# Setup work moved behind the first norm, value rows of the first image ahead of its depthwise product, and six of its first 16 stack transfers issued by GpSimd

## The reference

```python
# x = x + _L0_conv_ref(_ln_c(x), ...)
y = jnp.einsum('nchw,oc->nohw', x, cv1_w) + cv1_b[None, :, None, None]
t = y.transpose(0, 2, 3, 1)
v = (t @ vp_w.T + vp_b).reshape(B, H, W, G, GC)                 # values
dw = jax.lax.conv_general_dilated(y, dw_w, (1, 1), 'SAME', feature_group_count=C, ...)
dw = dw + dw_b[None, :, None, None]                             # depthwise 3x3
om = dw.transpose(0, 2, 3, 1) @ om_w.T + om_b                   # offsets and masks
...                                                             # split off, mask
d = _dcn_core(v, off, mask) @ op_w.T                            # bilinear samples of v at 9 taps
z = d @ cv2_w.T
z = (z - bn_m) * (bn_g / jnp.sqrt(bn_v + EPS)) + bn_b
z = z * jax.nn.sigmoid(z)
```

## Time and profile before

| What | Value |
|---|---|
| Median of 3 runs | 918.97 us (918.94 to 920.76) |
| The profiled execution, its own time | 918.25 us |
| Its span | 916.4 us |
| PE busy | 599.2 us (65%) |
| DVE busy | 538.9 us (59%) |
| ACT busy | 322.0 us (35%) |
| POOL busy | 465.7 us (51%) |
| First tap product on PE starts | 51.88 us |
| First add on POOL starts | 57.86 us |
| Mean granted clock of TensorE | 0.743 |

### The profile page before, as it was taken

The page is one execution under the profiler, slowest core; times in us unless marked ns, Lnnn a source line. Parts: engine busy times, 40 slices in busy tenths (PEclk is TensorE's granted clock), DMA queues, the critical chain, the costliest instruction groups (busy, mean ns, idle before and its releaser), DMA issues.

```text
span 916.4 us, 10354 instructions
## 1 busy us (share of the span) xinstructions
PE 599.2 (65%) x3032; PEld 446.3 (49%) x3032; DVE 538.9 (59%) x1018; ACT 322.0 (35%) x536; POOL 465.7 (51%) x364
## 2 busy tenths in 40 slices
PE   1566878787878787761288888873867771656511
PEld 0445556565656565640265665652656661445300
DVE  3257878797969796962366566552564654444411
ACT  2435352525252525100154554551232320433400
POOL 0058988899989998996100000004575733000075
PEclk9967575758585858555599999986686875677755
DMA  9463526565556562600445455410010101445311
GB/s 359 145 151 80 144 58 150 167 146 171 142 163 151 168 145 68 151 0 23 153 129 160 151 159 171 147 45 15 12 30 23 30 15 33 128 129 138 100 33 37
DMA packets 67013, 101.22 MB, mean 110 GB/s; under 512 B 25742, under 2 KB 45198, under 8 KB 66958
## 3 DMA queue, kind: packets, MB, share of 16 engines
q1 hardware_dynamic: 62416, 93.07, 35.7%
q0 software_dynamic: 4096, 6.30, 2.6%
q10 hardware_dynamic: 446, 1.20, 0.4%
HBM read 37.67 MB, written 25.10 MB: 68 GB/s over the span
## 4 chain that ended last, share of the span: by engine, by line
PE 32%; DVE 19%; issue 18%; POOL 13%; ACT 9%; SPq 5%; DMA 4%; POOLq 0%; DVEq 0%; ACTq 0%
DVE sb_prod L1085 6%; POOL sb_yg L1382 5%; POOL xs L1363 5%; PE ps_pa L479 4%; PE ps_t L514 4%; PE ps_c L472 3%; PE ps_t L581 2%; PE ps_pb L599 2%; DVE sb_hats L1160 2%; DVE sb_hats L1071 2%; ACT sb_hats L859 2%; PE ps_t L582 1%; PE ps_t L590 1%; PE ps_t L589 1%; PE ps_c L499 1%
## 5 line engine op out<-in xcount | busy, mean ns | idle before, releaser
L1351 POOL TENSOR_TENSOR sb_acc<-sb_acc,sb_prod 128x1024 f32<-128x1024 f32 x128 | 300.2, 2376 | 12.0 <-DVE sb_prod L1085 11.7
L1382 POOL DMA_INDIRECT sb_yg<-ys,sb_jdx x64 | 61.4, 959 | 295.3 <-DMA ys<-sb_yt 277.3
L514 PE MATMUL ps_t<-sb_vbd,sb_hx 128*128 128x256 f32 x576 | 139.9, 391 | 69.9 <-DVE sb_prod L1085 57.8
L1085 DVE TENSOR_TENSOR sb_prod<-ps_t,sb_hy 128x1024 f32<-128x1024 f32 x128 | 153.6, 1216 | 41.7 <-PE ps_t L514 31.9
L514 PEld LDWEIGHTS ps_t<-sb_vbd,sb_hx 128*128 128x128 f32 x576 | 110.1, 267 | 100.2 <-DVE sb_prod L1085 70.1
L1363 POOL DMA_INDIRECT xs<-sb_xr,sb_idx x64 | 64.4, 1007 | 25.4 <-issue 15.8
L1213 DVE TENSOR_TENSOR sb_hid<-ps_t,sb_hid 114x512 f32<-114x512 f32 x69 | 46.4, 686 | 46.3 <-ACT sb_hid L880 41.0
L499 PE MATMUL ps_c<-sb_dwT,sb_omx 128*128 128x256 f32 x144 | 53.5, 527 | 14.8 <-DVE sb_hats L1071 10.2
L880 ACT ACTIVATE sb_hid<-ps_t 114x512 f32<-114x512 f32 x69 | 41.2, 599 | 48.0 <-PE ps_t L582 47.9
L499 PEld LDWEIGHTS ps_c<-sb_dwT,sb_omx 128*128 128x128 f32 x144 | 34.9, 259 | 23.3 <-issue 17.4
L479 PE MATMUL ps_pa<-sb_ypad,sb_diag 128*64 128x256 f32 x96 | 40.8, 599 | 8.2 <-ACT sb_yrep L781 8.2
(11 more groups left out here) (253 smaller groups left out, 1294.2 us busy)
## 6 DMA issues: line engine op xcount, KB each, us to landing
sb_hx<-sb_hats SPq DMA_DIRECT2D x384, 96.0 KB, 2.2
xs<-sb_x3t SPq DMA_DIRECT2D x32, 512.0 KB, 6.1
sb_acc<-in_wcat SPq DMA_DIRECT2D x16, 876.0 KB, 4.5
sb_yrep<-in_wcat SPq DMA_DIRECT2D x7, 876.0 KB, 4.5
sb_nt<-xs SPq DMA_DIRECT2D x32, 128.0 KB, 2.1
sb_acc<-in_ucat SPq DMA_DIRECT2D x22, 160.0 KB, 2.4
sb_xt<-xs SPq DMA_DIRECT2D x23, 128.0 KB, 2.2
ys<-sb_yt SPq DMA_DIRECT2D x16, 128.0 KB, 2.4
```

The costliest lines, as they stand in the source:

```text
L514: last = mm(tb[u % 2][:, j * 256:(j + 1) * 256], hx[q % 3][:, j, o:o + P], vbd[n % 2][:, j * 256:(j + 1) * 256], start=True, stop=True)
L1085: v.tensor_tensor(o.rearrange("p (g c q) -> p g c q", g=G, q=H), tb[u % 2][:, :].rearrange("p (g c q) -> p g c q", g=G, q=H), w, ALU.mult) ...
L1351: g.tensor_tensor(acc[n % 2][:, t, :], acc[n % 2][:, t, :], prod[a % 3][:, :], ALU.add).then_inc(s_pool_acc, 1)
L1382: g.indirect_dma_start(out=yg[b][:, t, z, :], out_offset=None, in_=ys[0:NJT[m] * TILE, :], in_offset=bass.IndirectOffsetOnAxis(ap=jdx[m][: ...
```

## The change

Four things are changed.

1. **Setup behind the norm.** The making of `diag`, of `bns`, and the copies to `run` move into two steps, `fold` and `folded`, that stand behind `cv1` of image 0 in the list; ACT's square root is in `fold`. The fills that need no constant move ahead of DVE's wait for the constants. PE no longer waits for `s_set` at the start but at the first depthwise row; ACT and POOL wait for 4 in place of 5; DVE waits for 5 inside `fold`, and for the constants there too.
2. **Values first.** For image 0 alone, `value_rows` and `values` stand ahead of the three `depthwise_row`, `depthwise` and `offsets`.
3. **GpSimd issues.** Of the 16 stack transfers of image 0's first group, POOL issues part 2 (4 transfers, after `hath`) and half of part 3 (2 transfers, after `hatl`), on a semaphore of their own, `s_hp`. SP issues the other 10. PE waits for both before the first tap; ACT waits for both before it writes `hath[0]` again (group 2).
4. **Order strings.** ACT's string has one letter more, DVE's two, POOL's 24 (its new step `columns` returns at once for all groups but the first). Otherwise every engine's steps stand in the same order as before.

The strings are shown by their first lines; the rest of each is the same order moved along by the added letters.

```diff
     "act": """
-        aaaaaaaaaa aaaaaaaapa papaaappaa aaaappappa appaaaaaap pappaappaa aaaappappa appaaaaaap pappaappaa aaaappappa appaaaappp
+        aaaaaaaaaa aaaaaaaaap apapaaappa aaaaappapp aappaaaaaa ppappaappa aaaaappapp aappaaaaaa ppappaappa aaaaappapp aappaaaapp
...
     "dve": """
-        aaaaaaaaat taatattttt tttataaata tatattttaa ttpattpttp ttptttataa atatatattp aattatpttt ppttppptat taaatatata ttpttaattt
+        aaaaaaaaaa attaatattt tttttataaa tatatatttt aattpattpt tpttptttat aaatatatat tpaattatpt ttppttpppt attaaatata tattpttaat
...
     "pool": """
-        ttaatttttt tttttttttt attttptttt tttttttttt aptttptttt tpsttttttt pttattttpt ttttpstttt tttpttattt tptttttpst ttttttptta
+        ttaaaaaaaa tttttttttt ttttttaaaa ttttttpttt ttttttttta aaaptttptt tttpsttttt ttpttaaaat tttptttttp stttttttpt taaaattttp
...
@@ -75,8 +75,10 @@
 
     conv, taps, post = [], [], []
     for n in range(B):
-        conv += [("x_tokens", n), ("stats", n, 0), ("norm", n, 0), ("xn_channels", n), ("cv1", n), *(("depthwise_row", n, i) for i in range(3)),
-                 ("depthwise", n), ("offsets", n), *(("value_rows", n, i) for i in range(4)), ("values", n), *column_group(n, 0), ("row_distances", n, 0), ("row_distances", n, 1), ("row_weights", n, 0),
+        depthwise = [*(("depthwise_row", n, i) for i in range(3)), ("depthwise", n), ("offsets", n)]
+        value = [*(("value_rows", n, i) for i in range(4)), ("values", n)]
+        conv += [("x_tokens", n), ("stats", n, 0), ("norm", n, 0), ("xn_channels", n), ("cv1", n)] + [("fold",), ("folded",)] * (n == 0)
+        conv += (value + depthwise if n == 0 else depthwise + value) + [*column_group(n, 0), ("row_distances", n, 0), ("row_distances", n, 1), ("row_weights", n, 0),
                  ("row_weights", n, 1), *column_group(n, 1), *column_group(n, 2)]
         taps += [("tap", n, k, t) for k in range(K) for t in range(TT)]
         post += [("sampled", n), ("z", n), ("x1", n), ("stats", n, 1), ("norm", n, 1)] + routing(n, 0)[:-1]
@@ -288,6 +290,11 @@
         h3 = [tb[b][:, 512:1024] for b in range(2)]
         ca, cc = cb[:, 0:512], cb[:, 512:1024]
 
+
+        s_hp = sem("s_hp")
+
+        def landed(q):
+            return 256 * (q // 3 + 1) - 96 * (q % 3 == 0)
 
         s_const, s_zero, s_set = map(sem, ("s_const", "s_zero", "s_set"))
         s_bn, s_act_bn, s_pe_comb, s_act_comb = map(sem, ("s_bn", "s_act_bn", "s_pe_comb", "s_act_comb"))
@@ -364,9 +371,11 @@
                     sp.wait_ge(s_pe_t, TRI * TT * (q - 2))
                 sp.wait_ge(s_act_hh, 3 * q + 3)
                 for part, src in ((0, hath[b]), (2, hath[b]), (1, hatl[b]), (3, hatl[b])):
+                    if q == 0 and part == 2:
+                        continue
                     if part == 1:
                         sp.wait_ge(s_dve_hl, q + 1)
-                    for j in range(NJ):
+                    for j in range(NJ // 2 if q == 0 and part == 3 else NJ):
                         sp.dma_start(hx[s][32 * part:32 * part + 32, j, :].bitcast(f32),
                                      src[32 * j:32 * j + 32, :].bitcast(f32)).then_inc(s_hx[s], 16)
 
@@ -475,6 +484,8 @@
             def depthwise_row(n, i):
                 if i == 0:
                     pe.wait_ge(s_act_yr, n + 1)
+                    if n == 0:
+                        pe.wait_ge(s_set, 5)
                 for a in range(2):
                     last = mm(pa[0:C, 0:PIX], diag[:, 2 * i + a, :], ypad[:, i:i + H, 2 * a:2 * a + W], start=(i == 0 and a == 0),
                               stop=(i == 2 and a == 1))
@@ -504,9 +515,11 @@
                 u = UNITS * n + k * TT + t
                 q = NTRI * n + k // TRI
                 if t == 0 and k % TRI == 0:
-                    pe.wait_ge(s_hx[q % 3], 256 * (q // 3 + 1))
+                    pe.wait_ge(s_hx[q % 3], landed(q))
                 if k == 0 and t == 0:
                     pe.wait_ge(s_dve_v, n + 1)
+                    if n == 0:
+                        pe.wait_ge(s_hp, 96)
                 if u >= 2:
                     pe.wait_ge(s_dve_p, u - 1)
                 for j in range(NJ):
@@ -752,7 +765,6 @@
                      "xn2_channels": xn2_channels, "queries": queries, "keys": keys, "attn_values": attn_values, "k_tokens": k_tokens, "context": context, "q_channels": q_channels,
                      "mix": mix, "attend": attend, "nx": nx_channels, "nup": nup, "ndown": ndown, "nout": nout, "x4": x4}
             pe.wait_ge(s_const, n_const)
-            pe.wait_ge(s_set, 5)
             mm(pb[0:C, 0:C], op_[:, :], cv2[:, :], start=True, stop=True).then_inc(s_pe_comb, 1)
             walk("pe", steps)
 
@@ -763,11 +775,13 @@
             for dst, name in consts[1::2]:
                 act.dma_start(dst, A[name]).then_inc(s_const, 16)
             act.wait_ge(s_const, n_const)
-            act.wait_ge(s_bn, 1)
-            af(bns[:, 1:2], bns[:, 0:1], ACT.Sqrt).then_inc(s_act_bn, 1)
             act.wait_ge(s_pe_comb, 1)
             af(opcv[:, :], pb[0:C, 0:C], ACT.Copy).then_inc(s_act_comb, 1)
-            act.wait_ge(s_set, 5)
+            act.wait_ge(s_set, 4)
+
+            def fold():
+                act.wait_ge(s_bn, 1)
+                af(bns[:, 1:2], bns[:, 0:1], ACT.Sqrt).then_inc(s_act_bn, 1)
 
             def xn_channels(n):
                 act.wait_ge(s_pe_xnt, n + 1)
@@ -812,7 +826,9 @@
                 af(cb[:, 0:TRI * PIX], cb[:, 0:TRI * PIX], ACT.Relu, scale=-1.0, bias=1.0).then_inc(s_act_hh, 1)
                 act.wait_ge(s_act_hh, 3 * q + 2)
                 if q >= 2:
-                    act.wait_ge(s_hx[(q - 2) % 3], 256 * ((q - 2) // 3 + 1))
+                    if q == 2:
+                        act.wait_ge(s_hp, 96)
+                    act.wait_ge(s_hx[(q - 2) % 3], landed(q - 2))
                 af(hath[b][:, :], cb[:, 0:TRI * PIX], ACT.Copy).then_inc(s_act_hh, 1)
 
             def sampled(n):
@@ -954,7 +970,7 @@
                     act.wait_ge(s_out[n % 2], 16 * (n // 2))
                 af(outT[n % 2][:, :], pab[n % 2][0:C, 0:PIX], ACT.Copy).then_inc(s_act_o, 1)
 
-            steps = {"xn_channels": xn_channels, "cv1": cv1_bias, "values": values, "depthwise": depthwise, "row_distances": row_distances,
+            steps = {"fold": fold, "xn_channels": xn_channels, "cv1": cv1_bias, "values": values, "depthwise": depthwise, "row_distances": row_distances,
                      "columns": columns, "sampled": sampled, "z": z_silu, "x1": x1, "xf": xf_copy, "logits": logits, "slots": slots, "gates": gates,
                      "split": split, "nsplit": nsplit, "mx": mx_high, "up": silu, "mout": mout, "xn2_channels": xn2_copy,
                      "k_exp": k_exp, "v_copy": v_copy, "q_exp": q_exp, "k_tokens": k_tokens, "q_channels": q_channels, "nx": nx_high,
@@ -968,30 +984,35 @@
             v.memset(zero[:, :], 0.0).then_inc(s_set, 1)
             v.memset(ypad[:, :, :], 0.0).then_inc(s_set, 1)
             v.memset(yrep[C:P, :], 0.0).then_inc(s_set, 1)
-            dve.wait_ge(s_set, 3)
-            v.memset(yrep[C:C + 1, :], 1.0).then_inc(s_set, 1)
-            dve.wait_ge(s_const, n_const)
             for j in range(2):
                 v.memset(epst[:, j, :], (1e-6, 1e-5)[j])
             v.memset(mhalf[:, :], -0.5)
             v.memset(tilef[:, :], float(TILE))
             for m in range(2):
                 v.memset(xf[m][C:C + 1, :], 1.0)
-                v.tensor_copy(run[m][:, :], ebase[:, 0:NE[m]])
-            for i in range(3):
-                for a in range(2):
-                    last = v.tensor_scalar(diag[:, 2 * i + a, :], eye2[:, :], dww[:, 3 * i + 2 * a:3 * i + 2 * a + 1], None, ALU.mult)
-            last.then_inc(s_set, 1)
-            v.tensor_scalar(bns[:, 0:1], vecs[:, 5:6], 1e-5, None, ALU.add).then_inc(s_bn, 1)
-            dve.wait_ge(s_act_bn, 1)
-            v.reciprocal(bns[:, 0:1], bns[:, 1:2]).then_inc(s_bn, 1)
-            dve.wait_ge(s_bn, 2)
-            v.tensor_tensor(bns[:, 2:3], vecs[:, 2:3], bns[:, 0:1], ALU.mult).then_inc(s_bn, 1)
-            dve.wait_ge(s_bn, 3)
-            v.tensor_tensor(bns[:, 1:2], vecs[:, 4:5], bns[:, 2:3], ALU.mult).then_inc(s_bn, 1)
-            dve.wait_ge(s_bn, 4)
-            v.tensor_tensor(bns[:, 3:4], vecs[:, 3:4], bns[:, 1:2], ALU.subtract).then_inc(s_bn, 1)
-            dve.wait_ge(s_set, 5)
+            dve.wait_ge(s_set, 3)
+            v.memset(yrep[C:C + 1, :], 1.0).then_inc(s_set, 1)
+
+            def fold():
+                dve.wait_ge(s_const, n_const)
+                v.tensor_scalar(bns[:, 0:1], vecs[:, 5:6], 1e-5, None, ALU.add).then_inc(s_bn, 1)
+                for i in range(3):
+                    for a in range(2):
+                        last = v.tensor_scalar(diag[:, 2 * i + a, :], eye2[:, :], dww[:, 3 * i + 2 * a:3 * i + 2 * a + 1], None, ALU.mult)
+                last.then_inc(s_set, 1)
+                for m in range(2):
+                    v.tensor_copy(run[m][:, :], ebase[:, 0:NE[m]])
```

(38 more changed lines are left out.)

14 lines of the change are left out of this document (3 added, 11 removed).

## The result

Over 6 runs each, the changed kernel takes 916.09 us (913.48 to 917.97) and the kernel before 920.32 (918.94 to 921.45): ratio 0.9953, 95% interval 0.9934 to 0.9973. That is 4.2 us faster, somewhere between 2.5 and 6.1, and clear of 0.2%. Forecast were a gain of 4.6 (3.8 to 6) and a time of 914.4 (913 to 915.2, range 912.0 to 917.6). So the gain lies inside its span, while the time of 916.09 lies outside the inner one and inside the range: the kernel before came out at 920.32 here, where the forecast had started from 918.97. The profiled executions took 918.25 and 914.49, with spans of 916.4 and 912.6.

The account below looks back on a forecast made before the run. The prediction took a chain of stages, not one engine, to bound the kernel. From 918.97 us it took 3.49 (setup) and 1.43 (values first), added 0.3 (clock), zero for GpSimd's issues: 914.4, range 912.0 to 917.6.

Parts of the forecast that it names:

- The second table load: ACT's root, moved behind `yrep`, may bring another table load: 1.28 + 0.21 us, priced zero, 1.5 without cover.
- a loss of 0.3: Image 0's value rows and depthwise product, reordered under TensorE's clock: 9.2 us together against 8.92 before.
- The 1.66: Depthwise slowdown at the lower clock, 0.449 against 0.27 us each, used to price value rows at 0.183 to 0.206.
- the 1.55 of its one profile: Image 0's first columns at 34.21 us took 1.55 before the change, read as the clock having risen.
- +1.1: Gain forecast in us for the values-first order: 1.43 from the removed PE wait, less 0.3 for the clock.
- The sentence that weighed the Trainium skill: On image 0's order: whichever block comes first pays; total nears 12.4 us only if value rows lift the clock less readily.
- the 3.8 taken off SP: Moving 6 stack-transfer issues from SP to POOL saves SP 3.8 us that nobody waits for, so worth zero.
- The sum: Whole kernel: gains of 3.49 and 1.43 less 0.3 make 4.62 us, giving 914.4 us.
- the clock pays less back: Rival, 17%: value rows near 0.220 each or depthwise at low clock; gain 1.8 to 3.8 us, time about 916.
- rival in which the taps eat it: Head start at the first tap is lost in later steps: within 1.8 us of before, about 918; 8%.

Follow-up runs that it names:

- the warm runs: Runs of the changed kernel and of the kernel before with extra products of a zero tile in PE's idle time; ratios 0.9867 to 0.9952.
- setup only: The changed kernel without the values first and without GpSimd's issues; 915.37 us against 919.07, ratio 0.9964.
- GpSimd only: The kernel before with GpSimd issuing six of the first 16 stack transfers, nothing else; 919.22 us against 919.07, ratio 0.9996.
- no values first: The changed kernel with the old order of image 0, setup and GpSimd's issues kept; 915.89 us, ratio 0.9972.
- values only: The kernel before with image 0's value rows ahead of its depthwise product, nothing else; 920.23 us against 919.07, ratio 1.0020.
- SP all: The changed kernel with SP issuing all 16 first stack transfers; 916.00 us against 919.14, ratio 0.9964.
- GpSimd all: The changed kernel with GpSimd issuing all 16 first stack transfers; a single run, 918.64 us.
- the run with 18 products in place of 11: The changed kernel with extra zero products up to the taps, 18 in place of 11 before columns group 2; 905.75 us against 918.11, ratio 0.9867.
- the one slow profile: Slowest, profiled execution of the changed kernel with extra zero products (18 before columns group 2) and SP issuing all 16; that run's time 907.57 us, ratio 0.9873.

## Why the prediction was right, and where it was not

**Setup behind the norm: right.** 3.49 forecast; 3.59 by the rows from the constants to `yrep`, and 3.3 for this part alone. The second table load came, at 19.32 for 1.28, and was covered, as was every other piece that was moved. By the rows this part is the whole gain; by the times, 3.3 (1.9 to 4.6) against 4.2 (2.5 to 6.1), the two can't be told apart.

**Values first: the mechanism was right, the size and so the sign wrong.** The wait of 1.43 went away as forecast. The term "a loss of 0.3" for the clock was mis-sized, for three reasons. I scaled the value rows by the slowdown of wide products (1.66 to 1.87), where it is 1.9 to 2. The 1.66 itself came from four instructions of 0.27, while twelve at the higher level took 2.80 in the warm runs, 0.23 each. And I let the depthwise product run at the higher level from its first instruction (3.24); of the 9.1 to 9.8 that my own factors gave, I took the low end. Four profiles of each order with PE not warmed, read from the chain in order of time:

| | value rows + depthwise | first columns | stretch |
|---|---|---|---|
| depthwise first (before, setup only, GpSimd only, no values first) | 8.2 to 8.9, mean 8.5 | 1.5, 2.9, 2.9, 2.9 | 13.2 to 14.2, mean 13.8 |
| values first (after, values only, SP all, GpSimd all) | 10.9 to 12.2, mean 11.8 | 1.3 in each | 13.5 to 14.8, mean 14.4 |

The clock cost 3.3, not 0.3: the value rows take 0.22 each all the way, and the depthwise product behind them still ran partly or nearly wholly at the lower level. What I left out gives 1.2 back: with the old order the columns stand behind value rows and a wait, and ran at 2.9 three times out of four, while the prediction took the 1.55 of its one profile for the rule. In sum -3.3 + 1.4 + 1.2, about -0.6 before rounding, where +1.1 was forecast. The two rows of stretches overlap (13.2 to 14.2 and 13.5 to 14.8), so the -0.6 is weak; that there is no gain of 1.1 is not, and the values-first run alone was slower than the kernel before. The sentence that weighed the Trainium skill ("TensorE: Matmul & The Clock Gate", Part 1) named this outcome and I gave it 17%, with a time of about 916. The trace agrees with the page that the lower level is the resting state (7.09 cold, 3.79 warm), and the rows add that behind value rows alone the clock had not risen in any of the four profiles.

**GpSimd's issues: right at zero, prices wrong.** 0.56 for an issue, not 1.26: the indirect issue was the nearest row but not a near one. I gave each queue the landing time that it has alone, 2.2. With both issuing at once GpSimd's landed up to 4.2 after their issue and SP's up to 4.4, and the 3.8 taken off SP was 2.2. The last of GpSimd's landed at 42.6 and the last of SP's ten at 44.9, still 4.1 ahead of the first tap. (The prediction's landing times for SP, such as 50.6 before, count one step of 0.635 too many; it changes nothing there.) The stall beside DVE's copies, which the Trainium skill ("SBUF — State Buffer", SBUF: two separate sides) describes, did not show in the 16 issues of GpSimd issuing all, beside DVE instructions that read PSUM; no run here put a copy from SBUF to SBUF beside them.

**The sum** came out near by luck: 4.62 forecast, 3.0 by the mean rows (3.6 - 0.6), 4.2 measured between 2.5 and 6.1. One of its two gains, that of the order, had the wrong sign. The 4.2 rests on six runs of the kernel before with a median of 920.32; its later medians were 918.1 to 919.1, and against the 919.07 of 35 runs the changed kernel's 916.09 is 3.0 faster, outside the 3.8 to 6 forecast and inside the 1.8 to 3.8 of the rival "the clock pays less back". What the first tap gained stayed: no rival in which the taps eat it is seen, and the run with 18 products in place of 11 carried 1.5 at the first tap into 1.5 at the last add.

## What to carry to other kernels

When work is reordered on TensorE, price each block at the level of the clock at which it will then run, and take a narrow product's slowdown as the full factor of two (0.22 against 0.11 here). Look at what stands idle before it: products of zeros in PE's idle time bought as much on the kernel before (4.4 us) as the change did, and 5 to 8 more on top of it. And time taken off a queue is worth nothing until its last transfer is what somebody waits for, so compare landing times before moving issues, and expect transfers of two queues at once to land later than either does alone.

## What was not expected of the hardware

- The column of the granted clock reads 1.00 before its first change in a run, also where instructions run at the lower level: depthwise instructions of 0.449 us (at 22.53 in the kernel before) and value rows of 0.22 (at 19.36 in the changed one) stand under a 1.00. The durations tell the level.
- Value rows (64 columns against 128 x 128 weights) take 0.22 each at the lower level and 0.11 to 0.12 at the upper, a factor of 1.9 to 2; the columns product 1.53 and 2.90, a factor of 1.9.
- The constants land between 10.0 and 11.7 us after the start from one execution to the next, with the same transfers issued. The runs of one kernel spread over some 7 us; this and the clock (3.3 in the one slow profile) can be part of it, which no run isolates. A part worth 0.6 us could be read in rows only.
- A plain transfer's issue cost GpSimd 0.50 to 0.56 us and SP 0.635. Issued by one engine alone it landed 2.4 (GpSimd, 16 transfers) or 2.2 (SP, 16 transfers) after its issue; with both engines issuing at once, 2.9 to 4.2 and 2.2 to 4.4, and SP's own issues took up to 1.4 each.
